# Root, reciprocal and a Newton step in place of a power, and feed-forward parameters loaded during the convolution before

## The reference

```
x  = x + dwconv3x3(x) + pos_b
n  = (x - mean(x)) * rsqrt(var(x) + 1e-6) * ln1_g + ln1_b          # over the 64 channels
q, k, v = n @ q_w + q_b, (n @ k_w + k_b) * 8**-0.5, n @ v_w + v_b  # 8 heads of 8
a  = softmax(q kT + mask_w) v within rows, then softmax(q kT + mask_h) a within columns
x  = x + (a + dwconv5x5(v) + lepe_b) @ out_w + out_b
x  = x + gelu(layernorm(x, ln2_g, ln2_b) @ fc1_w + fc1_b) @ fc2_w + fc2_b   # 256 hidden, exact GELU
```

## Time and profile before

| | us |
|---|---|
| median of 3 runs (lowest, highest) | 2103.77 (2100.58, 2105.39) |
| the profiled execution | 2106.22 |
| its span in the profile | 2104.4 |
| first convolution | 0 to 318 |
| attention | 318 to 1565 |
| second convolution | 1565 to 1787 |
| projection and feed-forward | 1787 to 2104 |

### The profile page before, as it was taken

How to read it: one execution, slowest core, us unless ns; L and a number is a source line. 1 busy time by engine, 2 the same in 40 slices (tenths; PEclk the granted TensorE clock), 3 DMA queues, 4 the chain that set the end, 5 groups by cost and what they waited for, 6 DMA issues and landing times. The chain is left out here.

```text
span 2104.4 us, 89182 instructions
## 1 busy us (share of the span) xinstructions
PE 1852.3 (88%) x34510; PEld 1548.6 (74%) x34510; DVE 1428.2 (68%) x2270; ACT 1247.0 (59%) x2107; POOL 1173.6 (56%) x1858
## 2 busy tenths in 40 slices
PE   5877624999999999999999999999978995599998
PEld 5877522888887888877887877878768995477776
DVE  3588864777776777766777766767642663688885
ACT  4677734555555555564555555555544766488887
POOL 6477855554555554454555554555534001599997
PEclk8888755999999999999999999999988998799999
DMA  9589566678787787778787787776748994466663
GB/s 141 99 197 223 160 190 148 158 172 180 177 178 167 176 178 177 161 179 186 182 186 175 177 186 172 181 185 161 184 89 148 201 233 142 111 137 137 137 137 82
DMA packets 661152, 346.82 MB, mean 165 GB/s; under 512 B 562462, under 2 KB 613406, under 8 KB 660878
## 3 DMA queue, kind: packets, MB, share of 16 engines
q1 hardware_dynamic: 627782, 298.69, 65.1%
q0 software_dynamic: 31936, 43.83, 7.0%
q10 hardware_dynamic: 1160, 0.13, 0.1%
HBM read 105.42 MB, written 102.76 MB: 99 GB/s over the span
## 5 line engine op out<-in xcount | busy, mean ns | idle before, releaser
L813 ACT ACTIVATE att_prob<-att_st_ps 128x448 f32<-128x448 f32 x896 | 486.9, 544 | 439.0 <-PE att_st_ps L720 438.9
L888 DVE TENSOR_REDUCE att_mm<-att_s_ps 128x8 bf16<-128x448 f32 x896 | 556.2, 621 | 266.9 <-PE att_s_ps L690 263.2
L733 PEld LDWEIGHTS att_pv_ps<-att_vx,att_prob 128*56 128x56 f32 x14336 | 562.0, 132 | 89.2 <-issue 5.6
L733 PE MATMUL att_pv_ps<-att_vx,att_prob 128*56 128x18 f32 x14336 | 514.4, 202 | 5.8 <-ACT att_prob L813 4.3
L582 POOL DMA_DIRECT2D att_mvt<-att_mneg x256 | 136.3, 537 | 555.3 <-ACT att_mneg L802 484.9
L690 PE MATMUL att_s_ps<-att_kx,att_q_unit 120*56 120x448 bf16 x1792 | 347.2, 360 | 9.1 <-DMA att_q_unit<-att_qk_hi 7.4
L715 PE MATMUL att_st_ps<-att_mvt,set_both 122*56 122x448 bf16 x1792 | 345.7, 357 | 9.6 <-DMA att_mvt<-att_mneg 8.3
L720 PE MATMUL att_st_ps<-att_qx,att_k_hi 128*56 128x448 bf16 x1792 | 344.4, 356 | 0.0
L720 PE MATMUL att_st_ps<-att_qx,att_k_lo 128*56 128x448 bf16 x1792 | 342.1, 353 | 0.0
L573 POOL DMA_DIRECT2D att_qx<-att_q_hilo x512 | 245.8, 488 | 2.0 <-issue 1.7
L796 ACT ACTIVATE att_qk_hi<-att_pj,set_bias 128x392 bf16<-128x392 f32 x256 | 150.2, 587 | 124.9 <-PE att_pj L648 124.7
(11 more groups left out here) (209 smaller groups left out, 3196.4 us busy)
## 6 DMA issues: line engine op xcount, KB each, us to landing
att_xt<-xn_chunks SPq DMA_DIRECT2D x128, 196.0 KB, 3.4
att_k_hi<-att_qk_hi SPq DMA_DIRECT2D x128, 196.0 KB, 3.5
att_k_lo<-att_qk_lo SPq DMA_DIRECT2D x128, 196.0 KB, 3.8
att_qx<-att_q_hilo POOLq DMA_DIRECT2D x512, 49.0 KB
pos_x<-in_x_dram SPq DMA_DIRECT2D x128, 105.0 KB
lepe_x<-v_scratch SPq DMA_DIRECT2D x128, 105.0 KB, 4.2
x_scratch<-pos_x SPq DMA_DIRECT2D x128, 98.0 KB
xn_chunks<-pos_xrt SPq DMA_DIRECT2D x16, 784.0 KB, 5.2
```

The source lines that it names most:

```text
L733: ins = pe.matmul(pv_ps[v % 2][64 * h:64 * h + L, at:at + 18], prob[t % 4][:, 4 * h + a, :], vx[v][:, VW * j + 36 * a + 18 * h:VW * j + 36 ...
L813: act.activation(out, src, ACT.Exp).then_inc(exp_done, 1)
L888: dve.tensor_reduce(mm[v % 2][:, NH * j:NH * j + NH], s_ps[j % 2][:, 0:S8].rearrange("p (s k) -> p s k", k=L), AX.X, ALU.max).then_inc(max ...
```

## The change

Two parts. In the first convolution POOL no longer raises to the power -0.5. ACT takes the root of variance plus epsilon, DVE the reciprocal of that, r0, and POOL makes one Newton step: r0 * (1.5 - 0.5 * (var + eps) * r0 * r0), five instructions with a wait before four of them. The root of image n stands in ACT's list between its second and third copy of the convolution (at its end for the last batch), the reciprocal at the end of DVE's list for image n.

In the second convolution the sixteen parameter loads of the feed-forward stage stand in SP's list behind the attention loads of image 10 (`n == 7`). DVE's weight preparation is cut into steps at the end of its lists for images 0 and 9 to 15. The tiles for this are allocated before the second convolution, which also shares the two identity matrices. The feed-forward stage starts with its clears; SP loads the first four `rt` at once and the first four `x1` when four clears are done.

```diff
+class MlpSetup:
...
+    def parameters(self, sp):
+        par = self.par
+        for h in range(2):
+            p = slice(64 * h, 64 * h + 64)
+            sp.dma_start(self.wo_f[p, :], self.wo_d).then_inc(par, 16)
...
+            sp.dma_start(self.b1_in[:, h:h + 1], self.bf1_d[128 * h:128 * h + 128].unsqueeze(1)).then_inc(par, 16)
+        sp.wait_ge(self.bias_zero, 1)
+        for k in range(3):
+            sp.dma_start(self.bias_f[32 * k:32 * k + 1, 0, :], self.bo_d.unsqueeze(0)).then_inc(par, 16)
+        sp.dma_start(self.b2[:, :], self.bf2_d.partition_broadcast(128)).then_inc(par, 16)
...
+    def clear(self, dve):
+        dve.memset(self.bias_f[:, :, :].rearrange("p n c -> p (n c)"), 0.0).then_inc(self.bias_zero, 1)
+        self.done(dve.memset(self.ones_b[:, :], 1.0))
+        self.done(dve.memset(self.wo2[:, :], 0.0))
+        self.done(dve.memset(self.w12[:, :], 0.0))
+
+    def high(self, dve):
+        dve.wait_ge(self.par, 16 * 16)
+        self.done(dve.tensor_copy(self.wo1[:, :], self.wo_f[:, :]))
+        self.done(dve.tensor_scalar(self.w1_g[:, :], self.w1_f[:, :], self.g_c[:, 0:1], None, ALU.mult))
+        self.done(dve.tensor_copy(self.bias_p[0][:, :, :], self.bias_f[:, :, :]))
...
+    def weights(self, dve, n):
+
+        if n == 0:
+            self.clear(dve)
+        elif n == 9:
+            self.high(dve)
+        elif n == 10:
+            self.low_out(dve)
+        elif n == 11:
+            self.low_first(dve)
+        elif n == 12:
+            self.bias_rest(dve)
+        elif n == 13:
+            self.bias_last(dve)
+        elif n == 14:
+            self.bias_parts(dve)
+        elif n == 15:
+            self.settled(dve)
...
@@ conv_phase, sync
                     if n + 3 < B:
                         load_add(n + 3)
+                    if n == 7:
+                        mlp.parameters(sp)
@@ conv_phase, gpsimd
+            def inverse(n):
+
+                u = n % 2
+                var, r, r0 = st[u][:, 1, :], st[u][:, 2, :], st[u][:, 3, :]
+                pool.wait_ge(sd_done, n + 1)
+                pool.tensor_scalar(var, var, EPS, -0.5, ALU.add, ALU.mult).then_inc(eps_done, 1)
+                pool.wait_ge(eps_done, n + 1)
+                pool.wait_ge(flipped, n + 1)
+                pool.tensor_tensor(r, var, r0, ALU.mult).then_inc(newton, 1)
+                pool.wait_ge(newton, 3 * n + 1)
+                pool.tensor_tensor(r, r, r0, ALU.mult).then_inc(newton, 1)
+                pool.wait_ge(newton, 3 * n + 2)
+                pool.tensor_scalar(r, r, 1.5, None, ALU.add).then_inc(newton, 1)
+                pool.wait_ge(newton, 3 * n + 3)
+                pool.tensor_tensor(r, r, r0, ALU.mult).then_inc(rs_done, 1)
...
-                    pool.wait_ge(var_in, n + 1)
-                    pool.tensor_scalar(st[u][:, 1, :], st[u][:, 1, :], EPS, None, ALU.add).then_inc(eps_done, 1)
-                    pool.wait_ge(eps_done, n + 1)
-                    pool.tensor_tensor(st[u][:, 2, :], st[u][:, 1, :], half[:, :], ALU.pow).then_inc(rs_done, 1)
+                    inverse(n)
@@ conv_phase, scalar
+            def root(n):
+
+                u = n % 2
+                if n == 0:
+                    act.wait_ge(eps_set, 1)
+                act.wait_ge(var_in, n + 1)
+                if n >= 2:
+                    act.wait_ge(xn_done, n - 1)
+                act.activation(st[u][:, 2, :], st[u][:, 1, :], ACT.Sqrt, bias=eps[:, 0:1]).then_inc(sd_done, 1)
...
                     for cg in range(4):
                         conv_copy(b + 1, 4 * q + cg)
+                        if pos and cg == 1:
+                            root(n)
@@ conv_phase, vector
+            def flip(n):
+                dve.wait_ge(sd_done, n + 1)
+                if n >= 2:
+                    dve.wait_ge(rs_done, n - 1)
+                dve.reciprocal(st[n % 2][:, 3, :], st[n % 2][:, 2, :]).then_inc(flipped, 1)
...
                     if n >= 2:
                         col_copy(n - 2, range(2, G))
+                    flip(n)
...
                     if q < 2:
                         low(dve, n + q)
+                    mlp.weights(dve, n)
@@ mlp_phase, sync
-            sp.wait_ge(gaps, 1)
-            for v in range(NV - 1):
+            for v in range(4):
+                sp.dma_start(rt[v][:, :], rt_d[v]).then_inc(rt_in[v], 16)
+            sp.wait_ge(cleared, 4)
+            for v in range(4):
+                for r in range(2):
+                    sp.dma_start(x1[v][64 * r:64 * r + L, :, :], x1_v[v, r]).then_inc(x1_in[v], 16)
+            for v in range(4, NV - 1):
                 load(0, v)
@@ mlp_phase, vector
             for t in x1[0:4]:
-                done(dve.memset(t[32:64, :, :].rearrange("p j c -> p (j c)"), 0.0))
+                dve.memset(t[32:64, :, :].rearrange("p j c -> p (j c)"), 0.0).then_inc(cleared, 1)
             for t in (*o_ps[0:2], *y_ps):
-                done(dve.memset(t[:, :], 0.0))
...
+                dve.memset(t[:, :], 0.0).then_inc(cleared, 1)
+            dve.wait_ge(cleared, 8)
+            dve.sem_inc(ready, 1)
             dve.wait_ge(pre_pe, 1)
-            done(dve.tensor_tensor(b1[:, :], h_ps[0][:, 0:2], b1_in[:, :], ALU.add))
...
+            dve.tensor_tensor(b1[:, :], h_ps[0][:, 0:2], b1_in[:, :], ALU.add).then_inc(biased, 1)
             front(0, 0)
```

More of the change, by code:

```diff
@@ L991, in conv_phase @@
             xct = [sb(f"xct{u}", [128, W, H], BF16) for u in range(2)]
-            st = [sb(f"st{u}", [128, 3, NBLK], F32) for u in range(2)]
-            half = sb("half", [128, NBLK], F32)
+            st = [sb(f"st{u}", [128, 4, NBLK], F32) for u in range(2)]
+            eps = sb("eps", [128, 1], F32)
         else:
@@ L1216, in _ @@
             if pos:
-                pool.memset(half[:, :], -0.5).then_inc(half_done, 1)
-                pool.wait_ge(half_done, 1)
+                pool.memset(eps[:, :], EPS).then_inc(eps_set, 1)
             else:
@@ L1411, in _ @@
                 if pos:
+                    if b + 1 == NBATCH:
+                        root(n)
                     ahead(n + 1)
@@ L1576, in mlp_phase @@
         y_ps = [al.ps(f"y_ps{u}", [128, 512], F32) for u in range(2)]
-        par, zeroed, unit, prep, pre_pe, ready, half_done = (
-            sem(n) for n in ("par", "zeroed", "unit", "prep", "pre_pe", "ready", "half_done"))
+        cleared, biased, pre_pe, ready, half_done = (
+            sem(n) for n in ("cleared", "biased", "pre_pe", "ready", "half_done"))
         rt_in = [sem(f"rt_in{u}") for u in range(4)] * 2
@@ L1582, in mlp_phase @@
         out_st = [sem(f"out_st{u}") for u in range(2)] * 4
-        rs_done, lo_done, bias_zero, gaps = (sem(n) for n in ("rs_done", "lo_done", "bias_zero", "gaps"))
+        rs_done, lo_done = sem("rs_done"), sem("lo_done")
         o_done, t_done, fc1_done, fc2_done = (sem(n) for n in ("o_done", "t_done", "fc1_done", "fc2_done"))
@@ L1697, in _ @@
                 low(0, v)
-            pool.wait_ge(par, 16 * 16)
             def body(i, v, before, after):
@@ L1793, in high @@
                 act.activation(hl[v][:, :, 0:C], xc[v][:, :, :], ACT.Copy).then_inc(hi_done, 1)
-            act.wait_ge(ready, 1)
             def turned(i, v):
@@ L1861, in result @@
                                   x2[v][:, a:b, :], ALU.add).then_inc(out_sb, 1)
-            step = [0]
-            def done(ins):
-                step[0] += 1
-                ins.then_inc(prep, 1)
-            def settled():
-                dve.wait_ge(prep, step[0])
-            dve.memset(bias_f[:, :, :].rearrange("p n c -> p (n c)"), 0.0).then_inc(bias_zero, 1)
-            done(dve.memset(ones_b[:, :], 1.0))
-            done(dve.memset(wo2[:, :], 0.0))
-            done(dve.memset(w12[:, :], 0.0))
@@ L1885, in _ @@
-            settled()
-            done(dve.tensor_tensor(wo2[0:64, :], wo_f[0:64, :], wo1[0:64, :], ALU.subtract))
-            done(dve.tensor_copy(w11[:, :], w1_g[:, :]))
-            settled()
-            done(dve.tensor_tensor(w12[0:64, :], w1_g[0:64, :], w11[0:64, :], ALU.subtract))
-            done(dve.tensor_copy(bias_p[0][:, :, :], bias_f[:, :, :]))
-            settled()
-            done(dve.tensor_tensor(bias_r[0][:, :, :], bias_f[:, :, :], bias_p[0][:, :, :], ALU.subtract))
-            settled()
@@ L1894, in _ @@
-            done(dve.tensor_copy(bias_p[1][:, :, :], bias_r[0][:, :, :]))
-            settled()
-            done(dve.tensor_tensor(bias_r[1][:, :, :], bias_r[0][:, :, :], bias_p[1][:, :, :], ALU.subtract))
-            settled()
-            done(dve.tensor_copy(bias_p[2][:, :, :], bias_r[1][:, :, :]))
-            settled()
-            for k in range(3):
-                done(dve.tensor_copy(bias_3[32 * k:32 * k + 32, :, :], bias_p[k][32 * k:32 * k + 32, :, :]))
-            dve.wait_ge(pre_pe, 1)
@@ L1903, in _ @@
-            done(dve.tensor_tensor(b1[:, :], h_ps[0][:, 0:2], b1_in[:, :], ALU.add))
-            dve.wait_ge(unit, 1)
```

(16 more changed lines are left out.)

107 lines of the change are left out of this document (62 added, 45 removed).

## The result

The changed kernel runs in 2079.99 us (median of 4, 2076.21 to 2084.17) against 2103.81 for the kernel before (2100.58 to 2105.39): ratio 0.9889, 95% interval 0.9867 to 0.9911, so 1.1% faster, clear of the scatter of the runs. The forecast was 2071 with a range of 2064 to 2083. The profiled execution took 2080.0, its span is 2078.2, so 26.2 us were won there against 33.0 forecast.

| stage | before, us | after, us | won | forecast |
|---|---|---|---|---|
| first convolution (to attention's first load) | 318.4 | 297.4 | 21.0 | 23.7 |
| attention | 1247.0 | 1241.3 | 5.7 | 0 |
| second convolution | 221.4 | 231.3 | -9.9 | -0.6 |
| feed-forward | 317.7 | 308.3 | 9.4 | 9.9 |

A forecast was written before the change was run, and what follows sets the result against it. No engine bounds the first convolution; a loop through POOL's power does, 14.63 us an image. 23.7 (part 1) + 9.9 (feed-forward start) - 0.6 (second convolution) = 33.0 us off 2103.8 gives 2071; range 2064 to 2083.

The forecast's parts named there:

- 0.6 us on the path: Second convolution: four clears (0.35 us) delay batch 2's loads and one subtraction (0.25) stands between the last low halves.
- Image 11: Second convolution: parameter loads delay image 11's loads, a new DVE wait of 3 us, hidden from PE with 1 to 2 to spare.
- Part 1, the steps: First convolution, per image: five POOL steps 1.85 us, reciprocal 0.28, root about 0.3; two more table loads in all, off the path.
- The dear products: Rival, first convolution: POOL's products cost above 1.7 us each; at 4.83 each the kernel takes 2245 us; 2%.
- a table load at each root: Rival, first convolution: two ACT table loads of 1.28 us in each image, total 2083 us, or about 2107 at 2.66 each; 13%.
- Part 1, the cover: First convolution: DVE's next centring, 4 us, covers POOL's 1.5 us with 2.5 to spare, so the scale finds its factor ready.
- All of DVE's waits go: First convolution: DVE's 28.1 us of waits for the power go, less 4.5 for reciprocals and 1.5 at the last image: 22.1.
- The rival that DVE loses its gain to POOL's copies: First convolution: POOL's copies meet centring and scale, another 1.0 us in each of eleven images, 2082 us; 7%.
- The gate: First convolution: the last batch's inputs come late through SP's self-pacing chain of stores and loads; 4.1 us given back in ACT's queue.
- Border: First convolution, two batch borders: POOL clears the pads earlier, so DVE's waits for square and row copies go, 5.7 us won.
- Feed-forward start: Start of feed-forward: first addition at 1793.0 instead of 1802.90, 9.9 us won, with the first residual pair's landing ending the wait.

The follow-up runs named there:

- runs with pads: Unused bytes ahead of the second convolution's tensors: changed kernel with 32 or 160 bytes, stage 223.5 or 214.1 us; kernel before with 224 bytes, stage 226.6 us.
- Part 2 alone: Kernel before with only the feed-forward parameter loads and weight preparation moved into the second convolution; ratio 0.9995, no change.
- experiment 4: Changed kernel with 160 unused bytes ahead of the second convolution's tensors, input buffer on a multiple of 256; 2066.3 us, ratio 0.9815.
- experiment 9: Changed kernel with both convolutions' buffers on a multiple of 256 (96 and 160 unused bytes); 2056.6 us, ratio 0.9790.
- experiment 11: Changed kernel with both convolutions' buffers and every attention and feed-forward tensor on a multiple of 256 bytes; 2048.5 us, ratio 0.9742.
- The second Newton step: Changed kernel with four more POOL instructions of 128x28 an image; 2092.3 us, ratio 0.9948, last scale 11.7 us later than in the changed kernel.
- with their share at 0.58: Changed kernel with seven eighths of the first convolution's batch 3 input loads left out, same number of transfers; 2076.9 us, ratio 0.9868.
- experiment 6: Changed kernel with 96 unused bytes ahead of the first convolution's tensors, which then begin on a multiple of 256; 2073.5 us, ratio 0.9833.
- with the pads: Kernel before with both convolutions' buffers on a multiple of 256 (96 and 128 unused bytes); 2086.6 us, ratio 0.9938.

## Why the prediction was right, and where it was wrong

- **Time.** 2080 lies in the range, 9 us above the forecast and outside the forecast's own range of 2066 to 2076. The sum missed by 6.8 in the spans: +2.7 in part 1, +9.3 in the second convolution, +0.5 at the feed-forward start, and -5.7 in attention. Attention's 5.7 was luck: its code and place are the same in both kernels, and it took 1241.4 to 1249.8 us in kernels without part 2. Without it the profiled execution would have been 2085.7, outside the range.
- **The step that failed: "0.6 us on the path" in the second convolution.** The prediction put the stage down as TensorE's and its steady state as untouched, and it followed instructions and queues only. But in the trace of the kernel before, PE waits 18.6 us there for copies of rows that have to land first, so slower transfers lengthen the stage. Part 2 also moves tensors: it shifted the input buffer by 6,624 bytes, to a worse place, and the runs with pads give that 5 to 8 us. Part 2 alone came out at 0.9995. What remains when placement is equal is 2 to 3 us (223.5 against 221.0 and 221.4; 214.1 against 211.1; at 96 bytes 228.2 to 231.3 against 226.6), not 0.6. In the one pair followed, 1.6 of 3.0 was a lower granted clock in one group of matmuls. Whether the four clears and the subtraction cost their 0.35 and 0.25 no run shows; that the changed kernel is 0.6 longer behind batch 3's copies is no proof, since the clears stand before them.
- **Image 11.** The forecast wait of 3 us didn't come in the changed kernel. The attention loads at 1715.77 were image 11's and not image 10's: they wait for image 8's addition, which ends at 1715.7. Images 9 and 10 had gone out from 1706.5, and SP stood idle from about 1710. The parameters filled that gap. The reading was off by one image. The conclusion, hidden, held: even where the wait came (1.9 to 2.4 us, experiments 4, 9 and 11), PE's copies were ready in time in the kernel followed.
- **Part 1, the steps.** Products at 0.24 us and five steps in 1.6 (1.85 taken), reciprocal 0.316 (0.28 taken, so 5.1 and not 4.5 in all), root 0.315, two extra table loads off the path: right. The dear products and a table load at each root are out.
- **Part 1, the cover.** "All of DVE's waits go" was 2.9 us too much: 4.3 are left, of which the last image's 1.4 was forecast. Three products are stretched to about 2 us by the centring and the scale waits 0.84, 0.84 and 1.17 us. The second Newton step shows how narrow this is.
- **Port.** The rival that DVE loses its gain to POOL's copies was right in kind and small: the copies moved from scale to centring, net 1.6 us. The first scale comes 14.7 us behind the first centring instead of 13.0; 1.5 of this is the second image's centring, 3.50 us long instead of 2.03.
- **The gate.** Forecast 4.1, measured 4.54, from a chain that does pace itself, but not for the reason given, DMA engines at 91%: with their share at 0.58 the chain was 2.8 us shorter. It is paced by stores that are issued and have to land before the loads go. Overlooked: the same chain frees the row buffers, and the row copies wait for them in each of the three images before the gate, 10.3 us in all.
- **Border and gate together** were 5.7 won less 4.1 given back, 1.6 us net. Up to the last scale DVE waited 7.4 us for the square and the row copies before (5.4 and 2.0) and 7.8 after (2.6 and 5.2): the square's wait halved, and the row copies, late for their store, took back more. With the lost cover and the port this is what part 1's 21.0 lacks to 23.7; other small terms partly cancel.
- **A side sum.** The rival of loads in every image ended at 2107 by twelve images that lose 1.6 us each. From its own 14.6 and 16.8 us an image the loss is 2.2, which gives some 2109. It bears on nothing, since no such load came.
- **Feed-forward start.** 6.5 us after the barrier against 6.25, and the residual's landing ends last, as said.

Left open: where the aligned attention and feed-forward tensors save time, what share of the placement effect each kind of transfer has, and what sets attention to 1237 or 1251 us. The granted clock there is 0.97 or 0.98 in all profiles, and PE's busy time (1183 to 1194 us) varies less than the stage.

## What to carry to other kernels

A tensor allocated earlier moves all that come behind it. Where a stage waits for transfers, even a stage whose PE is busy 79% of the time, compare the start bytes of its buffers before and after a change, and compare kernels at equal placement: 32 bytes were worth 8 us in one stage, and two pads took the changed kernel from a ratio of 0.9889 to 0.9790, nearly as much as the change itself. A slow function on a shared path is worth replacing by short steps on three engines, but read beside which long instruction the short ones will fall. When stages that an edit leaves alone move by as much as the effect sought, profile each part alone before believing the sum.

## What the runs showed of the hardware

- Row loads of 256-byte pieces ran at three speeds by where their buffer starts in the partition: the second convolution took 228.2 to 231.3 us at 96 past a multiple of 256 in the kernels with part 2 (five kernels), 223.5 at 128 (one), 214.1 to 215.7 on the multiple (four). All tensors of the stage move with the buffer.
- SP's issue of the first convolution's plain stores follows the same: between 100 and 290 us a median of 779 ns at 160 past the multiple (changed kernel), 520 on it (experiment 6); over the whole stage in the kernel before 637 and, with the pads, 489:
```profile
L1233 SPq DMA_DIRECT2D x_scratch<-pos_x x104: 343/779/1995, 102.7 to 264.0; - x104
```
```profile
L1235 SPq DMA_DIRECT2D x_scratch<-pos_x x100: 343/520/1667, 99.7 to 251.4; - x100
```
- A POOL instruction of 0.24 to 0.29 us lasted 1.9 to 2.1 us where DVE's centring of 128x1792 ran beside it.
- A DMA busy share of 0.89 was no sign that the DMA engines set the pace: at 0.58 the chain of stores and loads took 44.7 us instead of 47.5.
- Attention, the same code in all kernels and the same placement in all but one, took 1237 to 1251 us from one execution to the next.
